# A selective-scan stage's six middle groups, written out or as a loop on each engine

## The reference

```
def _mamba_dir(x, inW, convW, convB, xpW, dtW, dtB, Alog, Dp, outW):
    xi, z = split(x @ inW.T)                       # 256 channels each
    u = silu(causal_conv4(xi) + convB)
    dt, Bm, Cm = split(u @ xpW.T)                  # 8, 16, 16
    delta = softplus(dt @ dtW.T + dtB)
    A = -exp(Alog)                                 # (256, 16)
    # for each t:  h = h * exp(delta_t * A) + (delta_t * u_t) * B_t ;  y_t = sum_n h * C_t
    y = (y + u * Dp) * silu(z)
    return y @ outW.T
y_fwd = _mamba_dir(x, ..._f)
y_bwd = flip(_mamba_dir(flip(x), ..._b))
return 0.5 * (y_fwd + y_bwd)
```

## Time and profile before

| | |
|---|---|
| time, median of 3 runs | 3135.29 us (3132.32 to 3135.34) |
| the profiled execution: its time, its span | 3135.29 us, 3133.5 us |
| busy in the span: PE, DVE, ACT, POOL | 2302.1, 2205.0, 1556.3, 1421.3 us |
| mamba stage, groups i = 1 to 6 | 1769.6 to 2485.6 us |

### The profile page before, as it was taken

The page is one execution under the profiler, slowest core; times in us unless marked ns, Lnnn a source line. Parts: engine busy times, 40 slices in busy tenths (PEclk is TensorE's granted clock), DMA queues, the critical chain, the costliest instruction groups (busy, mean ns, idle before and its releaser), DMA issues. The chain is left out here.

```text
span 3133.5 us, 55056 instructions
## 1 busy us (share of the span) xinstructions
PE 2302.1 (73%) x20075; PEld 1452.6 (46%) x20075; DVE 2205.0 (70%) x3826; ACT 1556.3 (50%) x2529; POOL 1421.3 (45%) x1127
## 2 busy tenths in 40 slices
PE   4888656764777769899968989988988975552703
PEld 2555445553555535555534545545545543341303
DVE  4887546886677735555527788888888884888698
ACT  4888525552677732222226666666665652221460
POOL 4555334555222200000008888888988982322001
PEclk9999877886799989999979999999999987665856
DMA  1000010000000010000022222222222220000000
GB/s 39 1 0 0 8 31 16 15 15 4 1 0 0 0 46 1 0 0 0 1 59 63 78 73 69 79 73 68 85 72 66 77 69 30 15 13 8 0 0 27
DMA packets 109830, 94.33 MB, mean 30 GB/s; under 512 B 12256, under 2 KB 106352, under 8 KB 109552
## 3 DMA queue, kind: packets, MB, share of 16 engines
q1 hardware_dynamic: 109680, 92.26, 9.8%
HBM read 83.32 MB, written 2.62 MB: 27 GB/s over the span
## 5 line engine op out<-in xcount | busy, mean ns | idle before, releaser
L1939 POOL TENSOR_TENSOR mam_h<-mam_h,mam_c_all 128x1024 f32<-128x1024 f32 x256 | 644.2, 2528 | 102.6 <-DVE mam_h L2011 102.2
L2011 DVE TENSOR_TENSOR_SCAN mam_h<-mam_decay,mam_ps_b 128x1024 f32<-128x1024 f32 x256 | 574.2, 2275 | 145.8 <-PE mam_ps_b L1642 144.5
L1642 PEld LDWEIGHTS mam_ps_b<-mam_diag,mam_duT 64*128 64x128 f32 x4096 | 250.4, 190 | 253.2 <-DVE mam_h L2011 157.5
L1642 PE MATMUL mam_ps_b<-mam_diag,mam_duT 64*128 64x128 f32 x4096 | 293.7, 286 | 92.4 <-DVE mam_h L2011 80.9
L1833 ACT ACTIVATE mam_decay<-mam_delta,mam_a_neg 128x508 f32<-128x508 f32 x512 | 330.3, 709 | 35.4 <-DVE mam_h L2011 35.3
L1661 PE MATMUL mam_ps_y<-mam_h,all_ident 64*64 64x512 f32 x2048 | 264.7, 634 | 9.9 <-POOL mam_h L1939 9.9
L519 DVE TENSOR_REDUCE at_top<-at_ps_s 128x4 f32<-128x512 f32 x256 | 175.0, 683 | 123.1 <-PE at_ps_s L359 123.1
L1234 ACT ACTIVATE moe_silu<-moe_ps_g 128x512 f32<-128x512 f32 x144 | 86.0, 597 | 291.0 <-PE moe_ps_g L1181 262.3
L437 ACT COPY at_probT<-at_ps_t 128x512 f32<-128x512 f32 x256 | 144.9, 588 | 121.4 <-PE at_ps_t L344 121.1
L198 POOL TENSOR_TENSOR at_parts_rest<-at_qk,at_parts 128x256 f32<-128x256 f32 x64 | 42.8, 668 | 321.4 <-ACT at_parts L193 321.4
L1184 PE MATMUL moe_ps_u<-moe_ynT,moe_w_up 128*128 128x512 f32 x288 | 159.8, 638 | 35.7 <-DVE moe_hidden L1317 35.7
(11 more groups left out here) (348 smaller groups left out, 4981.7 us busy)
## 6 DMA issues: line engine op xcount, KB each, us to landing
mam_c_all<-mam_c_rows SPq DMA_DIRECT2D x256, 256.0 KB, 3.4
all_x_all<-in_x SPq DMA_DIRECT2D x8, 256.0 KB, 4.5
ret_xg<-all_x_all SPq DMA_DIRECT2D x32, 64.0 KB, 1.8
ret_ctx<-in_ctx SPq DMA_DIRECT2D x32, 64.0 KB, 1.9
mam_xg<-all_x_all SPq DMA_DIRECT2D x8, 256.0 KB, 4.2
xat_xg<-all_x_all SPq DMA_DIRECT2D x8, 256.0 KB, 2.4
xat_ctx<-in_ctx SPq DMA_DIRECT2D x8, 256.0 KB, 2.9
out<-qua_res SPq DMA_DIRECT2D x8, 256.0 KB, 2.3
```

The lines of the kernel that those rows point to most:

```text
L1642: last = nc.tensor.matmul(ps_b[:, slot, odd, :, at // 2, x:x + HT], duT[r, d, s % DT, at, :], diag[r, chunk % SLOTS, at, :, :], start=True ...
L1939: nc.gpsimd.tensor_tensor(flat(h[:, slot, :, :, :, :]), flat(h[:, slot, :, :, :, :]), flat(c_all[:, chunk, :, :, :, :]), ALU.mult).then_in ...
L2011: nc.vector.tensor_tensor_scan(row(h[:, s % H_SLOTS, :, :, :, :]), row(decay[:, s % SLOTS, :, :, :, :]), row(ps_b[:, s % 2, :, :, :, :]), ...
```

## The change

On each of the five engines the Python `for` over the middle groups becomes a hardware loop. The bodies are the same text; `group(i, ...)` is now emitted once, with i in a register, and the engine jumps back at its end.

```
@@ sync
-            for i in range(1, NG - 2):
+            with sp.Fori(1, NG - 2) as i:
                 group(i, True)
@@ tensor
-            for i in range(1, NG - 1):
+            with pe.Fori(1, NG - 1) as i:
                 assert group(i, True).n == PER
@@ scalar
-            for i in range(1, NG - 1):
+            with act.Fori(1, NG - 1) as i:
                 group(i, True)
@@ gpsimd
-            for i in range(1, NG - 1):
+            with pool.Fori(1, NG - 1) as i:
                 group(i, True)
@@ vector
-            for i in range(1, NG - 1):
+            with dve.Fori(1, NG - 1) as i:
                 steps = Steps(dve, dve_steps, i * per_loop + HEAD + FIRST - per_loop, per_loop)
                 group(i, True, steps)
                 steps.closed()
```

## The result

The changed kernel takes 3152.36 us (median of 6 runs, 3150.87 to 3164.57) beside 3132.21 (3126.98 to 3135.34) for the kernel before on the same chip: the ratio is 1.0073, 95% interval 1.0054 to 1.0091, so it is slower, by 0.5 to 0.9%. Its profiled execution, which is not one of the six, took 3142.05 us, span 3140.3. The first scan of mamba comes 6.9 us earlier in it than in the profile of before, and group 0 took 3.1 us less; the change touches neither. So I compare the groups i = 1 to 6, from one first scan to the next.

The account below looks back on a forecast made before the run. The mamba stage was taken as paced by hand-overs among PE, DVE and POOL, no engine full. Terms 6.0 + 3.2 + 2.3 + 7.0 = 18.5 us on 3135.3 gave 3153.8, predicted as 3154 us, range 3134 to 3173.

Parts of the forecast that it names:

- Term A: DVE scans behind a settle at s = 9 to 11: register wait values cost 0.20 us at 30 starts, 6.0 us.
- term B: DVE scans released by PE: making `y_done`'s wait value delays 66 starts, 3.2 us, ends 0 and 13.2.
- Term C: PE's `b_rows` behind `h_ready`: making `diag_ready`'s value delays 36 starts, 2.3 us, ends 0 and 7.2.
- Term D: PE's five jumps back: fetching instructions takes 3.4 us, partly covered by `sum_states`; 7.0 us, ends 0 and 17.
- first rival: Mamba loops: register work stays hidden and no fetch shows, so the time stays at 3135 us; chance 0.17.
- Register work hidden: Mamba loops: register operations cost nothing, as in attention, and no fetch shows; 3135 us, chance 0.17.
- PE's body kept: PE's loop body stays in the core, wait values cost as forecast, 11.5 us; 3147 us, chance 0.15.
- Faster by the order of DVE and POOL: At s = 9 log1p step and multiply swap order, the multiply gaining 0.9 us, 11 us in all; 3124, chance 0.08.

Follow-up runs that it names:

- e10: Kernel before with DVE, ACT, POOL and SP looping, PE written out, and four products computed a second time in each direction: 3125.12 us, 0.9982.
- e9: Kernel before, all groups written out, with four matrix products computed a second time in each direction to fill PE's idle time: 3125.62 us, 0.998.
- e11: Changed kernel with a hint ahead of PE's jump and four products computed a second time in direction 1 alone: 3126.65 us, 0.9996.
- e3: Changed kernel, all five engines looping, with PE's loop starting each pass with a hint that names its jump: 3134.16 us, 1.0013.
- e1: Changed kernel with PE's groups written out; the other four engines loop: 3131.94 us, 0.9999 of the kernel before.
- e2: Kernel before with only PE looping, the other four engines written out: 3144.68 us, 1.0054.
- e4: Changed kernel with two groups in each pass of PE's loop, so PE jumps twice, not five times: 3139.42 us, 1.0024.
- e6: Changed kernel, no hint, with PE's body shortened from 2,009 to 1,657 matrix instructions by leaving out parts of the computation: 3123.75 us, 0.9975.
- e8: Changed kernel with jump hint, DVE's late scan waits ahead of the settle, and four products computed a second time in each direction: 3137.74 us, 1.0028.
- e5: Changed kernel with jump hint and DVE's waits for the scans at s = 9 to 11 moved ahead of the settle: 3137.04 us, 1.0018.

## Why the prediction came out as it did

The time, 3152, is the forecast's 3154; beside its own reference it grew by 20.1 us, and the six groups grew by 18.1 us in the profile, where the sum said 18.5. That the sum agrees is luck. The terms inside were not right:

| per six groups, us | forecast | measured |
|---|---|---|
| A and B, registers of DVE | 6.0 + 3.2 | 5.9 (e10 less e9, 0.98 a group) |
| C, registers of PE | 2.3 | 4.4 (e11 less e10, 0.73 a group) |
| D, the jump back | 7.0 | 16.5 (5 times 122.96 less 119.34, less 1.6 for the stretch that group 2 still has at its end) |
| half-clock stretches of before that are gone | not seen | -8.7 (716.0 less 6 x 117.62, less the same 1.6) |
| sum | 18.5 | 18.1 |

The measured column closes because group 1 of the changed kernel (119.34) and e11's groups (119.33) take the same; that is no separate proof of each row.

*Term A* held in place and size: the five scans that it names are those that fell behind, by 0.2 us each, 5.9 us over the six groups. That leaves nothing for *term B*, its lower end. *Term C* is 4.4 us, above the middle that I took and within its ends, but not where I put it. I spread it over 36 starts. Scan by scan, e11 falls behind e10 by 0.21 us at the first scan of each direction, whose `b_rows` has a third wait ahead of it (`copied`), and by 0.08 at three others. The same 0.7 us stands between e3 and e1 without any fill, and between e2's group 1 and that of before, where both have the stretch. (e11 is filled in one direction only, and its clock still falls in direction 0. That costs nothing there: e9's groups 1 and 2, with and without such a stretch, both take 117.62, and e11's groups 1 and 2, with one and with two, 119.3.)

*Term D* is mis-sized, 16.5 us for 7.0, just inside its upper end of 17. The cover was there as I put it: `sum_states` ran its 1.95 us over the start of the fetch. But I took 3.4 us for the fetch, from the landing time of a data DMA. The trace has a record of the jump instruction itself: taken, it lasts 3.34 to 4.20 us, 3.83 on the mean. Of that `sum_states` covers 1.83, and the first product comes 0.30 after it, so PE stood idle for 2.3 us on the mean (11.5 over five), not 1.4. And I didn't count what follows: the scans fall behind by another 1.0 to 1.15 us after the idle time in the groups 3 to 6. The clock falls there, but it isn't the whole of it: in group 2 and in e4's two groups, where it doesn't fall at the jump, 0.6 to 0.85 us follow as well. So the clock's share is 0.6 us a jump at most; what the rest is I have not found. I also said about 8 packets a group; it was 10.

*What was missing* is the clock. I had read the granted clock of whole groups, 0.96, and not asked where in a group it is lost. 1.6 us of each group before was a stretch at 1.2 GHz ahead of the last scan, and groups 3 and 5 lost 0.4 us more in direction 0. The changed kernel's groups 1, 3, 4, 5 and 6 don't have the stretch at the end, and that gave back most of what the registers cost. So term D was 9.5 us too small, and 8.7 us that no term had were taken off again. Without D the terms gave 3147; e3, which has no gap at the jump, took 3134. That is my first rival's time, but not for that rival's reason: in e3's profile the register work isn't hidden, its time came back from the clock.

*The rivals.* "Register work hidden" is refuted in the profiles, group 1 of the changed kernel among them, by e10 and e11; their medians don't decide it. "PE's body kept" is refuted by the packets, and e6 shows where it would hold. "Faster by the order of DVE and POOL" didn't occur: the long log1p steps take 3.17 us (3.27 before) and the multiplies beside them 3.25 (3.26). Open is why the stretch leaves a group whose gap is as long as before; that filling PE's idle time takes it away is shown, what exactly decides it is not. Open too is how much of the register work stands in an average execution, between 0 and 10 us.

## What to carry to other kernels

Before a long body becomes a loop, count the instructions of its longest engine. If the trace shows none of that size kept, expect each pass to begin with a fetch, and what it costs to be more than its idle time. A hint ahead of the jump or a shorter body avoids it; the hint must be looked at again when the body changes, and it has its price where the loop ends. In a stage paced by hand-overs, look for the places where the granted clock is below 1 before adding up small delays: a delay of 1 us can be given back, and a gain of 1 us taken, by a half-clock stretch that moves. And where PE waits for 2 us and the clock falls behind the wait, a useless product in it can be worth more than a useful instruction saved elsewhere.

## What the runs showed of the hardware

- A taken jump to instructions that are no longer in the core left PE idle for 1.8 to 3.7 us after 1.95 us of queued products (12 jumps of the changed kernel, e2 and e4); with 1,657 matrix instructions in the body there was no packet and no gap (e6). PE's jump instruction is recorded with 3.3 to 5.2 us in the former, 0.21 in e6, 0.36 to 0.39 with the hint (e3), 1.4 to 2.0 in e8, and 0.08 where the loop ends and it isn't taken.
- With the hint, a body of 2,009 matrix instructions had no gap at the jumps (e3) and 9 packets a group; with 2,017 (e11) the same; with 2,025 (e8) a gap of 0.6 to 2.2 us came back a little behind each jump, with 10 or 11 packets. Where the hinted loop ends, PE stood idle for 2.9 us (e3), 3.15 (e5) and 1.75 (e11), but not in e8.
- Between a settle and the next scan, waits on register values cost 0.18 to 0.25 us; issued ahead of the settle they cost nothing (e5).
- PE at 1.2 GHz behind a gap of 2.08 us in the kernel before, and at 2.4 GHz behind one of 2.27 us in e3.
